# Block 0's indices, stack and first tiles by another chain of transfers, and whole first tiles in layers 0 and 1

## What is computed

```python
e = stack([tbl_f[ids[:, f]] for f in range(39)], axis=1)     # 1024 x 39 x 16
x0 = xk = e
for l, (W, b) in enumerate(((w0, b0), (w1, b1), (w2, b2))):  # W: 39 x fields(xk) x 128
    z = relu(einsum('bhd,bkd,hks->bsd', x0, xk, W) + b[None, :, None])
    if l < 2:
        xk = z[:, :64, :]
        direct.append(z[:, 64:, :])
    else:
        direct.append(z)
logit = sum(concatenate(direct, axis=1), axis=-1)            # 1024 x 256
h = concatenate([logit, dense_ctx], axis=1)
y = relu(relu(h @ W_top1 + b_top1) @ W_top2 + b_top2) @ W_top3
```

## Time and profile before

| | |
|---|---|
| median of 3 runs | 1244.64 us (1243.7 to 1245.4) |
| the profiled execution | 1244.94 us, span 1243.1 us |
| busy | PE 1179.9, DVE 1061.9, POOL 1002.6, ACT 580.7 us |
| TensorE's first matmul; its first of layer 1 in step 0 | 52.88; 71.39 us |
| SP's issue of the second transfer of block 0's rows | 1.32 us |
| E in steps 0, 1 and 2 | 103.07, 174.94, 246.82 us |

### The profile page before, as it was taken

The page is one execution under the profiler, slowest core; times in us unless marked ns, Lnnn a source line. Parts: engine busy times, 40 slices in busy tenths (PEclk is TensorE's granted clock), DMA queues, the critical chain, the costliest instruction groups (busy, mean ns, idle before and its releaser), DMA issues.

```text
span 1243.1 us, 14868 instructions
## 1 busy us (share of the span) xinstructions
PE 1179.9 (95%) x3856; PEld 726.5 (58%) x3856; DVE 1061.9 (85%) x927; ACT 580.7 (47%) x563; POOL 1002.6 (81%) x629
## 2 busy tenths in 40 slices
PE   0289999999999999999999999999999999999999
PEld 0155666656565665656566565656656565666665
DVE  2278998989899898989889898998989898998984
ACT  1145444444545444454544445454444545444545
POOL 6678897998889899888989888888988889765651
PEclk9999999999999999999999999999999999999999
DMA  4785726365472626556262745637274563627000
GB/s 125 242 256 191 223 63 218 125 182 201 157 226 60 218 108 206 177 172 211 84 204 97 225 159 172 211 102 215 79 233 140 172 211 123 212 72 231 9 1 1
DMA packets 110269, 196.21 MB, mean 158 GB/s; under 512 B 52975, under 2 KB 64334, under 8 KB 110249
## 3 DMA queue, kind: packets, MB, share of 16 engines
q1 hardware_dynamic: 100009, 193.33, 47.2%
q0 software_dynamic: 10240, 2.64, 2.0%
HBM read 193.36 MB, written 12.78 MB: 166 GB/s over the span
## 4 chain that ended last, share of the span: by engine, by line
PE 69%; POOL 13%; DVE 8%; issue 6%; ACT 2%; DMA 2%; POOLq 0%; SPq 0%; DVEq 0%; ACTq 0%
PE acc L845 67%; POOL lo L464 7%; POOL emb L454 6%; DVE prod L706 3%; DVE lo L719 2%; ACT hi L556 2%; DVE acc L706 1%; DVE hi L716 1%; DMA x_tiles<-x_rows 0%; DMA x_rows<-x_rows 0%; DVE xk L706 0%; PE acc L925 0%; POOLq L163 0%; DMA x_rows<-emb 0%; ACT xk L522 0%
## 5 line engine op out<-in xcount | busy, mean ns | idle before, releaser
L706 DVE TENSOR_TENSOR prod<-x_tiles,xk 128x1024 f32<-128x1024 f32 (+2 forms) x643 | 757.5, 1215 | 123.9 <-PE acc L845 83.4
L464 POOL TENSOR_TENSOR lo<-prod,hi 128x1024 fp32r<-128x1024 f32 (+1 forms) x288 | 690.5, 2400 | 141.1 <-ACT hi L556 136.4
L845 PE MATMUL acc<-prod,wfull 128*128 128x512 f32 (+2 forms) x1408 | 660.6, 593 | 0.0
L556 ACT ACTIVATE hi<-prod 128x1024 fp32r<-128x1024 f32 (+1 forms) x291 | 308.4, 1060 | 406.3 <-DVE prod L706 322.4
L845 PE MATMUL acc<-hi,whi 128*128 128x512 f32 (+1 forms) x800 | 353.0, 441 | 57.7 <-ACT hi L556 57.6
L845 PEld LDWEIGHTS acc<-prod,wfull 128*128 128x128 f32 (+2 forms) x1408 | 266.8, 189 | 205.7 <-issue 177.4
L454 POOL DMA_INDIRECT emb<-table,block_idx x320 | 308.6, 964 | 69.3 <-issue 63.9
L845 PE MATMUL acc<-lo,whi 128*128 128x512 f32 (+1 forms) x736 | 316.1, 517 | 2.4 <-POOL lo L464 1.2
L845 PE MATMUL acc<-hi,wlo 128*128 128x512 f32 (+1 forms) x800 | 316.1, 395 | 0.0
L845 PEld LDWEIGHTS acc<-hi,whi 128*128 128x128 f32 (+1 forms) x800 | 150.9, 189 | 112.4 <-issue 72.2
L845 PEld LDWEIGHTS acc<-lo,whi 128*128 128x128 f32 (+1 forms) x736 | 138.3, 190 | 133.2 <-issue 104.0
(11 more groups left out here) (72 smaller groups left out, 163.4 us busy)
## 6 DMA issues: line engine op xcount, KB each, us to landing
x_tiles<-x_rows SPq DMA_DIRECT2D x304, 512.0 KB, 5.1
x_rows<-x_rows SPq DMA_DIRECT2D x16, 624.0 KB
x_tiles<-x_rows SPq DMA_DIRECT2D x32, 256.0 KB, 5.6
x_stack<-x_rows SPq DMA_DIRECT2D x48, 156.0 KB
emb<-table,block_idx POOLq DMA_INDIRECT x320, 3.8
x_rows<-emb SPq DMA_DIRECT2D x16, 152.0 KB, 3.3
x_tiles<-w SPq DMA_DIRECT2D x1, 768.0 KB, 6.1
x_tiles<-w SPq DMA_DIRECT2D x1, 704.0 KB, 8.6
```

The costliest lines, as they stand in the source:

```text
L464: nc.gpsimd.tensor_tensor(lo[0:r, product_slot(j), :], prod[0:r, product_slot(j), :], hi[0:r, part_slot(j), :].bitcast(f32), ALU.subtract) ...
L556: nc.scalar.activation(hi[0:r, part_slot(j), :], held(n, parity, j)[0:r, :], ACT.Copy).then_inc(hi_ready, 1)
L706: nc.vector.tensor_tensor(held(n, parity, j)[0:r, :], in0, in1, ALU.mult).then_inc(product_ready, 1)
L845: mm = nc.tensor.matmul(z[:, c], w[0:r], part[0:r, c], start=first and i == 0, stop=last and i == len(weights) - 1)
```

## The change

1. `KINDS[0]` goes from GFFGFFF to FGFFGFF and the first five tiles of layer 1 from GFDGF to FGDGF, so both layers begin with a whole tile. `SQUARE` follows the tile with shift 0 in the staged weights, whose load is cut in two.
2. Block 0's indices and their bases come by two small loads of 20 columns, one on SP's queue and one on ScalarE's. GpSimd adds these and gathers; the add over all blocks comes behind these gathers.
3. A small buffer `x0_head` in HBM gets the 39 rows and the first two again (`write_head`, three transfers behind `write_rows`). ScalarE waits for it and loads the stack of block 0 from it; SP repeats the rows and goes on to the tiles.
4. VectorE makes the `wlo` of layers 1 and 2 only when block 0's rows are written.

```diff
--- before.py
+++ after.py
@@ -60,7 +60,7 @@
 HI_AT, HI2_AT, LO_AT, COPY_AT = 0, 32, 64, 96
 DENSE_ROWS = LO_AT + DIM
 
-KINDS = ["GFFGFFF", "GFDGF" * 2 + "GFHGF" + "GFDGF", "GFFGF" + "GFFGD" + "GFHGF" + "GFDGF"]
+KINDS = ["FGFFGFF", "FGDGF" + "GFDGF" + "GFHGF" + "GFDGF", "GFFGF" + "GFFGD" + "GFHGF" + "GFDGF"]
 SHORT = 12
 TILES = [list(range(T0)),
          list(range(T0)) + list(range(T0, T0 + 5)) + [TWIN] + list(range(T0 + 5, TWIN)),
@@ -69,6 +69,7 @@
 assert all(k.count("H") == 1 and k[SHORT] == "H" for k in KINDS[1:])
 SPLITS = [[t for t, k in enumerate(ks) if k in "GD"] + [t for t, k in enumerate(ks) if k == "H"] for ks in KINDS]
 FULLS = [[t for t, k in enumerate(ks) if k == "F"] for ks in KINDS]
+SQUARE = (SPLITS[0] + FULLS[0]).index(0)
 SPLIT_AT = [0, len(SPLITS[0]), len(SPLITS[0]) + len(SPLITS[1])]
 FULL_AT = [0, len(FULLS[0]), len(FULLS[0]) + len(FULLS[1])]
 N_SPLIT = sum(map(len, SPLITS))
@@ -160,6 +161,8 @@
 
     x0_rows = nc.dram_tensor("x0_rows", [BLOCKS, SROWS, COLS], f32, kind="Internal").ap()
 
+    x0_head = nc.dram_tensor("x0_head", [FIELDS + 2, COLS], f32, kind="Internal").ap()
+
     with ExitStack() as ctx:
         def sb(name, shape, dt=f32):
             return ctx.enter_context(nc.sbuf_tensor(name, shape, dt))
@@ -172,6 +175,7 @@
 
         rows_idx = sb("rows_idx", [128, BLOCKS * PAIRS], i32)
         base_sb = sb("base_sb", [128, BLOCKS * PAIRS], i32)
+        first_base = sb("first_base", [128, PAIRS], i32)
         block_idx = [sb(f"block_idx{p}", [128, PAIRS], i32) for p in range(2)]
         emb = [sb(f"emb{p}", [128, PAIRS * DIM]) for p in range(2)]
         stack_at = nc.sbuf_base
@@ -225,6 +229,8 @@
         top2 = x0_tiles[:, own:own + TILES2, :]
         y_sb = x0_tiles[0:1, own + 3, :]
 
+        first_ids_loaded = sem("first_ids_loaded")
+        head_written = sem("head_written")
         ids_loaded = sem("ids_loaded")
         idx_added = sem("idx_added")
         idx_ready = sem("idx_ready")
@@ -309,11 +315,12 @@
                 sp.dma_start(w_stage[0:ROWS0, 0:n, :], w0[:, 0:n, :]).then_inc(w0_loaded, 16)
                 sp.dma_start(w0f_stage[0:ROWS0, 0:len(FULLS[0]) - 1, :], w0[:, n:T0 - 1, :]).then_inc(w0_loaded, 16)
                 sp.dma_start(w0f_stage[0:LAST0, len(FULLS[0]) - 1, :], w0[0:LAST0, T0 - 1, :]).then_inc(w0_loaded, 16)
-                sp.dma_start(w0t_stage[0:ROWS0, 1:T0 - 1, :], w0t[:, 1:T0 - 1, :]).then_inc(w0_loaded, 16)
+                sp.dma_start(w0t_stage[0:ROWS0, 0:SQUARE, :], w0t[:, 0:SQUARE, :]).then_inc(w0_loaded, 16)
+                sp.dma_start(w0t_stage[0:ROWS0, SQUARE + 1:T0 - 1, :], w0t[:, SQUARE + 1:T0 - 1, :]).then_inc(w0_loaded, 16)
                 sp.dma_start(w0t_stage[0:LAST0, T0 - 1, :], w0t[0:LAST0, T0 - 1, :]).then_inc(w0_loaded, 16)
 
                 sp.wait_ge(w0_cleared, 1)
-                sp.dma_start(w0t_stage[FIELDS:ROWS0, 0, :], w0t[FIELDS:ROWS0, 0, :]).then_inc(w0_loaded, 16)
+                sp.dma_start(w0t_stage[FIELDS:ROWS0, SQUARE, :], w0t[FIELDS:ROWS0, SQUARE, :]).then_inc(w0_loaded, 16)
                 for l, b in enumerate((b0, b1, b2)):
                     sp.dma_start(bias[:, l:l + 1], b).then_inc(bias_loaded, 16)
                 for l, w in ((1, w1), (2, w2)):
@@ -381,12 +388,24 @@
                     sp.dma_start(x0_tiles[:, slot, :], rows_ap(m, SHIFT[tile], [[COLS, 128], [1, COLS]])
                                  ).then_inc(tile_loaded[slot], 16)
 
+            sp.dma_start(block_idx[0][:, :], ids[:, 0:PAIRS]).then_inc(first_ids_loaded, 16)
             sp.dma_start(rows_idx[:, :], ids).then_inc(ids_loaded, 16)
             sp.dma_start(base_sb[:, :], base).then_inc(ids_loaded, 16)
             load_weights()
+            def write_head():
+
+                row = lambda r, dims: bass.AP(x0_head.tensor, r * COLS, dims)
+                sp.dma_start(row(0, [[DIM, 128], [2 * COLS, PAIRS - 1], [1, DIM]]),
+                             emb[0][:, 0:(PAIRS - 1) * DIM].rearrange("p (i d) -> p i d", d=DIM)
+                             ).then_inc(head_written, 16)
+                sp.dma_start(row(FIELDS - 1, [[DIM, BLOCK], [1, DIM]]),
+                             emb[0][0:BLOCK, (PAIRS - 1) * DIM:PAIRS * DIM]).then_inc(head_written, 16)
+                sp.dma_start(row(FIELDS, [[DIM, 128], [1, DIM]]), emb[0][:, 0:DIM]).then_inc(head_written, 16)
+
             write_rows(0, 0)
+            write_head()
             repeat_rows(0)
-            load_stack(0)
+            sp.wait_ge(rows_repeated, 16)
             for tile in range(T1):
                 if tile_slot(0, tile) == SLOTS - STAGED:
 
@@ -444,6 +463,9 @@
                                       ).then_inc(idx_ready, 1)
 
                 pool.wait_ge(idx_ready, m + 1)
+                if is_step(m, 2):
+
+                    pool.wait_ge(head_written, 3 * 16)
                 if reuse:
 
                     pool.wait_ge(rows_written, 2 * 16 * (m - 1))
@@ -464,11 +486,14 @@
                 nc.gpsimd.tensor_tensor(lo[0:r, product_slot(j), :], prod[0:r, product_slot(j), :],
                                         hi[0:r, part_slot(j), :].bitcast(f32), ALU.subtract).then_inc(lo_ready_g, 1)
 
+            pool.wait_ge(first_ids_loaded, 32)
+            nc.gpsimd.tensor_tensor(block_idx[0][:, :], block_idx[0][:, :], first_base[:, :], ALU.add
+                                    ).then_inc(idx_ready, 1)
+            pool.wait_ge(idx_ready, 1)
+            gather(0, 0, PAIRS)
             pool.wait_ge(ids_loaded, 32)
             nc.gpsimd.tensor_tensor(rows_idx[:, :], rows_idx[:, :], base_sb[:, :], ALU.add).then_inc(idx_added, 1)
             pool.wait_ge(idx_added, 1)
-            take_indices(0, 0, reuse=False)
-            gather(0, 0, PAIRS)
             take_indices(1, 1, reuse=False)
             gather(1, 0, 12)
 
@@ -607,6 +632,8 @@
                                      ).then_inc(y_ready, 1)
 
 
+            act.dma_start(first_base[:, :], base[:, 0:PAIRS]).then_inc(first_ids_loaded, 16)
+
             act.sem_inc(z_evacuated[2], 1)
             for l in range(3):
 
@@ -615,6 +642,10 @@
                 nc.scalar.activation(whi[0:r, SPLIT_AT[l]:SPLIT_AT[l] + n, :],
                                      w_stage[0:r, SPLIT_AT[l]:SPLIT_AT[l] + n, :], ACT.Copy).then_inc(whi_ready, 1)
             act.wait_ge(bias_loaded, 48)
+
+            act.wait_ge(head_written, 3 * 16)
+            for g in range(PER):
+                act.dma_start(x0_stack[g * FIELDS:(g + 1) * FIELDS, :], x0_head[g:g + FIELDS, :]).then_inc(stack_loaded, 16)
             copy_stack(PROLOGUE)
             round_hi(PROLOGUE, 1, L0, L2)
             evacuate(0, 0, accumulator(0, 1), T0, reuse=False)
@@ -668,11 +699,11 @@
 
         @block.vector
         def _(dve):
-            nc.vector.memset(w0t_stage[:, 0, :], 0.0).then_inc(w0_cleared, 1)
+            nc.vector.memset(w0t_stage[:, SQUARE, :], 0.0).then_inc(w0_cleared, 1)
             nc.vector.memset(direct2[:, :], 0.0).then_inc(direct2_cleared, 1)
             dve.wait_ge(direct2_cleared, 1)
 
-            dve.wait_ge(w0_loaded, 6 * 16)
+            dve.wait_ge(w0_loaded, 7 * 16)
             n, f = len(SPLITS[0]), len(FULLS[0])
             nc.vector.tensor_tensor(wfull[0:ROWS0, 0:f - 1, :], w0f_stage[0:ROWS0, 0:f - 1, :],
                                     w0t_stage[0:ROWS0, n:T0 - 1, :], ALU.add)
@@ -684,6 +715,9 @@
             for l in range(3):
 
                 dve.wait_ge(whi_ready, l + 1)
+                if l == 1:
+
+                    dve.wait_ge(rows_written, 32)
                 part = slice(SPLIT_AT[l], SPLIT_AT[l] + len(SPLITS[l]) - (l > 0))
                 r = rows(l, 0)
                 if l:
```

## The result

| | before | changed |
|---|---|---|
| median | 1245.23 us (6 runs) | 1250.80 us (1250.41 to 1252.08, 6 runs) |
| ratio to before | | 1.0047, 95% interval 1.0034 to 1.006 |
| profiled execution, span | 1244.94, 1243.1 us | 1251.01, 1249.1 us |

The change costs 5.6 us. The forecast was a cost of 8.6 us (1253.2 after 1244.64): the direction is right and the time lies inside the range, but the cost was forecast half as large again. The two halves of the forecast can be read apart in the new trace.

A forecast was written before the change was run, and what follows sets the result against it. TensorE, busy 748.56 of 750 us mid-run, was taken as the bound, with GpSimd's unbroken run setting the period. Start -5.65 - 0.5 - 1.0 = -7.15 and steps +15.7 gave +8.5: 1253.2 us after 1244.64, range 1248 to 1257.5.

The forecast's parts named there:

- Layer 0's order: In each of 14 steps GpSimd's run starts 1.12 us later, period 73.0: cost 15.7 us (14.8 to 16.8).
- Layer 1's order: Layer 1's first five tiles: no cost in the steps, 1.0 us won at layer 1's start.
- The start: Before the steps: first product at 44.8 after 50.43, gain 5.65; with later terms -7.15 us (-2.1 to -8.9).
- the index chain: Block 0's index loads: first gather at 4.2 instead of 6.23, gain 2.0 us (1.1 to 2.6).
- from the first write to the first product: Stack loaded from its own small buffer, tiles straight behind the repeat: net gain 1.7 us (-0.4 to 2.3).
- The `wlo` term: Block 0's gathers: two long ones beside VectorE's subtractions give back 1.95 us once these move (bound: nothing).
- Whole tiles first: TensorE starts behind a product, not a `hi`: net gain 0.5 us in the prologue, 1.0 at layer 1's start.
- The sum: Whole kernel: start -7.15 and steps +15.7, together +8.5 us, span 1251.6 after 1243.1.
- rival 1: In the steps GpSimd's run is not delayed or catches up; only the start's gain is left: 1237.5 us, chance 0.08.
- The second (the start nearly lost): Head's writes and stack's loads delay the repeat by 2.8 us, lower index gain: start -4.1, 1256.2 us, chance 0.14.
- The third (half hides): In the steps half the cost hides, 7.7 us against the start's 7.15: about 1245 us, chance 0.06.

The follow-up runs named there:

- orders-only one: Both new tile orders put into the kernel before, none of the new transfers: 1256.75 us, ratio 1.0095.
- run with spread gathers: Layer 2's eight gathers stand behind its first six G tiles, not four: 1239.07 us in the kernel before, 1231.38 us in the changed kernel.
- `wlo` early: Changed kernel without VectorE's wait for the written rows before layers 1 and 2's `wlo`: 1252.16 us, ratio 1.0061.

## Why the prediction was right

**Layer 0's order.** Predicted: run at E + 4.45, 1.12 us late, period 73.0, 15.7 us in 14 steps. Measured: E + 4.33, 1.00 late, period 72.81, 14 x 0.94 = 13.2. The mechanism, the engine, the order on ScalarE, the unbroken run and the number of steps were all as put. The term was mis-sized by 0.18 in each step, and both 1.00 and 0.94 lie below the lower bound of 1.06 that was given for it (14.8 us): 0.12 because ScalarE starts the `hi` 0.09 us ahead of the end of `direct` (171.84 before 170.82 + 1.11 = 171.93), where a gap was taken, and the rest because TensorE was 0.1 us faster in this step from the end of the wait to the next E (42.17 us after 42.27); why it was is not shown. TensorE's stall, predicted at 1.8, is 2.77 - 1.32 = 1.45 read the same way, and 0.2 at the small wait before it.

**Layer 1's order.** Predicted at nothing in the steps and 1.0 at the start; 71.81 to 71.85 and 72.81 to 72.84 with and without it, and 1.07 at the start. Right.

**The start.** Predicted first product 44.8, measured 43.48. The profiled execution of before was a late one: in the two other kernels with all of the old chain the first product came at 49.34 and 49.48, in the orders-only one at 49.11, and in the seven with all of the new chain (the changed one among them) from 43.36 to 44.87. Means are 49.6 of four (with 50.43) and 44.0 of seven: 5.6 us, for 5.65 in the prediction. That the means meet it so closely is luck, since inside it the terms moved: the index chain won 2.87 us in this pair and some 2.4 against the other old chains (first gather 5.71 to 5.90) for 2.0, because the small load landed after 2.0 us and the gather followed the add after 0.28 and not 0.9. From block 0's first gather to its last the means say 1.65 for 1.95 (25.68 and 24.03 us), and from the first write to the first product 1.4 for 1.7 (15.6 and 14.2). The `wlo` term failed as a constant: it depends on where the gathers stand when the subtraction begins.

**Whole tiles first.** 0.5 predicted for the prologue, 0.36 measured (first product to first evacuation 15.95 us after 16.31), 1.06 and 1.07 at layer 1's start. The end of the prologue is GpSimd's, as put: TensorE waits there for the second subtraction (54.53 to 56.9) and goes on at 56.94.

**The sum.** -7.15 + 15.7 = +8.5 predicted; -7.27 + 13.2 = +5.9 measured, +6.0 by the spans, +5.6 by the medians. What is off is the step's 2.5 us. That the start's 7.27 stands so near to 7.15 is luck as well: it is 8.4 us at layer 1's first matmul, less 1.1 that layer 1 took longer, and the prediction had neither. The start's outer bounds do not add up either: the terms as given make -2.2 and -8.35, not -2.1 and -8.9.

**Where TensorE's wait was over-read.** The prediction took 0.70 us as TensorE's idle time in a step, from start to start. The run with spread gathers shows that only 0.4 of it was a loss (71.87 - 71.47), and in the changed kernel 1.40 (72.81 - 71.41) where starts said 1.45 and a small 0.2 earlier. It did not enter the sum, which only shifts the run; it did enter rival 1's reserve and three expectations. Start to start over-counts: a `lo` pair that had to wait is done sooner once it starts (0.58 us from 204.55 to the matmul behind the pair, 0.86 from 196.28, where it stands straight behind a whole tile). Counted from the whole tile to the matmul behind the pair, the wait before was 2.60 - 2.18 = 0.42 us. The trace of before had this answer without any run: its last period, the one without gathers and without the stall, goes from 1109.22 to 1180.69, which is 71.47 us. In the changed kernel the last one is 71.41.

**The rivals.** The first (GpSimd catches up) has no room: the run had no gap in any trace, and an evacuation of 1.1 us moved alone cost 1.03 in each step. The second (the start nearly lost) saw a real cost, 0.9 us of SP's issues ahead of the repeat, but not its size; the stack's data cost the repeat nothing that shows. The third (half hides) is out by the period.

## What to carry to other kernels

Before an order of work is changed, look for the engine whose run sets the period, and ask what starts that run; here one rounding on a third engine, at a hand-written place that counted tiles by position and not by kind. Read behind the first bound at once: the one behind it was 0.25 us away, and mending the first won 3 us of 13, while taking three gathers out of the run won 19. Take the cost of a wait from the work behind it and not from the distance of two starts, or from a kernel without it.

## What the runs showed of the hardware

TensorE's clock. It idled 4.7 us between prologue and layer 1 before, and 3.6 in the changed kernel. Busy time by stretch of the changed kernel (length, then each engine's busy time with its count, PEclk, DMA share, GB/s):

```profile
61.00:63.00 2.00, 0.00 (x0) 0.00 (x0) 1.27 (x2) 1.71 (x2) 0.96 (x2) 0.66 1.08 395
63.00:65.00 2.00, 2.00 (x3) 0.96 (x4) 2.00 (x2) 0.88 (x1) 0.00 (x0) 0.50 0.99 375
65.00:67.00 2.00, 2.00 (x4) 0.88 (x3) 2.00 (x3) 1.82 (x3) 1.75 (x1) 0.50 1.03 399
67.00:69.00 2.00, 2.00 (x7) 1.62 (x6) 2.00 (x3) 0.43 (x1) 1.85 (x3) 0.63 1.05 261
```

and of the kernel before:

```profile
70.00:72.00 2.00, 0.60 (x2) 0.51 (x3) 2.00 (x3) 1.09 (x2) 0.58 (x1) 0.78 1.03 389
72.00:74.00 2.00, 2.00 (x5) 1.32 (x4) 2.00 (x3) 1.34 (x2) 1.85 (x2) 0.50 1.07 221
74.00:76.00 2.00, 2.00 (x6) 1.05 (x5) 2.00 (x3) 0.73 (x1) 1.98 (x2) 0.86 1.08 112
```

The granted clock is 0.50, the 1.2 GHz level, in both. In this pair the shorter idle time was followed by the longer stretch at it: layer 1 ran about 5.5 us at half clock (63.0 to 68.5), and 3.2 before (71.4 to 74.5). From its first matmul to E0 layer 1 took 32.79 us after 31.68, which is the 1.1 us that the start lost again. But the idle time does not settle it: over all 13 kernels layer 1 ran 3.1 to 4.0 us at the low level in the five that idled 4.7 us, and 3.4 to 6.0 in the eight that idled 3.6, four of them 3.4. From layer 1's first matmul to E0 it was 31.60 to 32.09 us in the five and 32.03 to 33.08 in the eight: in the mean half a microsecond of the gain of 1.07 was lost again. What decides was not tried.

A gather that starts while VectorE works on two SBUF operands takes longer than its usual 0.94 us. The subtractions for `wlo` (1.63 and 1.49 us) made it 1.2 to 2.4 us in every kernel, wherever they stood, and the sums of layer 0's weights made it up to 1.41. In all 13 kernels a gather that began at least 0.08 us behind the start of such an operation ended 0.81 to 0.83 us behind its end, or after its usual 0.94 us where that was later: in the changed kernel 8.50 + 1.41 = 9.91 after 8.41 + 0.69 = 9.10, and 35.71 + 1.56 = 37.27 after 34.83 + 1.63 = 36.46. A gather that began before the operation, or up to 0.05 us behind its start, lost nothing by it (20.94 beside 20.96 with `wlo` early). VectorE's products, whose second operand `xk` lies in PSUM, did not do this: of the 282 gathers from 72 us on in the kernel before none took 1 us. The Trainium skill, in "SBUF — State Buffer", section "SBUF: two separate sides", has VectorE with two SBUF inputs and GpSimd lock each other out of a shared pair of ports, and whichever starts first keeps it for its whole instruction. The trace agrees where VectorE is first. Where the gather is first it does not show such a lock: the subtraction at 34.83 began 0.4 us into the gather at 34.43 and took its usual 1.63 us.
